# Attention stage: reductions over two PSUM banks, and a score ring of three banks in place of two pairs

## The chip, the cores and the metric

The kernel runs on one core of one Trainium2 chip. The metric is device time in microseconds; the kernel before took 2791.23 us (median of three runs, 2777.22 to 2791.93).

## The reference, cut to what matters

Sixteen images of 32 channels and 56 x 56 pixels go through a convolution block, a single-head self-attention over the 3136 pixels of each image, and a small mixture-of-experts layer. The change touches the attention alone:

```python
def _L1_attn_ref(x, Wq, bq, Wk, bk, Wv, bv):
    q = jnp.einsum('bsd,de->bse', x, Wq) + bq
    k = jnp.einsum('bsd,de->bse', x, Wk) + bk
    v = jnp.einsum('bsd,de->bse', x, Wv) + bv
    scores = jnp.einsum('bqd,bkd->bqk', q, k) / jnp.sqrt(d)
    attn = jax.nn.softmax(scores, axis=-1)
    return jnp.einsum('bqk,bkd->bqd', attn, v) + x
```

## The kernel before, in words

Three stages follow one another: `prepare` (convolutions, and the stacks of keys and queries, written to device memory), `attend`, and `finish` (value projection, experts, output). `attend` is the part of the change.

Per image the scores are laid out with keys on partitions: 24 full chunks of 128 keys and one of 64 (`NF` = 24), against seven tiles of 448 queries (`TILE`). Four kinds of work make up the stage.

- **Scores** (`scores`, matmuls on L1158): one matmul of 128 x 128 weights and 448 columns per chunk and tile, into the tensor `psS`. It holds four PSUM banks as two pairs; a pair is filled by two matmuls, and one ScalarE instruction over 896 columns (`exponentials`, L1248) takes the exponential of both and writes the ring `PR` in SBUF.
- **Maxima** (`maxima`, matmuls on L1182): the row maximum of the scores is needed ahead of the exponential, so the scores are computed a second time, with queries on partitions. Two matmuls that use 64 array rows each run beside each other, into two banks out of the three of `psX`; VectorE reduces each bank (448 columns) with an instruction of its own (L1331). An image has 172 such units, taken as 86 pairs. They run 32 pairs ahead of the scores (`LEAD`).
- **Sums** (`sums`, L1200): the exponentials times the values, four chunks at a time in four column strips of 32, fp32, accumulated in `psV`. Two matmul records stand for each product, eight for a step. At the end of a query tile four small products with the half chunk are added (L1207), and ScalarE copies `psV` out (`keep`, L1255).
- **Half chunks** (`half_scores`, L1147, and `half_exponentials`, L1241): the last 64 keys of two query tiles in one bank. They use a bank of the score pairs in turn. `max_parts` (L1342) and `turn_max` (L1192, L1350) bring the maxima of a part of an image into a row that the score matmuls subtract.

A **step** is four chunks of one query tile; an image has 42 steps, the stage 672. The order on TensorE is written out by hand in the last loop of its block. Each engine runs its instructions in order and waits on semaphores: `s_full` (scores there), `p_ready` (exponential done, so the bank is free), `x_full` and `x_done` for the maxima, `p_used` for the ring `PR`. The order of a step before is:

```python
scores(n, s, 0)                # two matmuls, one pair of banks
maxima(*pairs[0])
sums(*divmod(q, STEPS))        # of two steps earlier
half_scores(n, s // PSTEPS)    # only in 4 of 42 steps
maxima(*pairs[1])
scores(n, s, 1)                # the other pair
```

So the second pair of scores of a step and the first of the next stand together, four matmuls in a row. Of the 672 steps 625 hold two pairs of maxima, 31 hold three and one holds one; the last 15 hold none. A score pair waits until the exponential of the pair two places back is done; a pair of maxima waits until all but the last reduction of those issued ahead of it are done.

Of the kernel before, what the change touches and what calls it, by code (L numbers as in the profile page):

```python
# [10 lines left out]
ALU = mybir.AluOpType  # L11
# [935 lines left out]
def attend(nc, wts, scr, fin):  # L947
# [3 lines left out]
    with ExitStack() as ctx:  # L951
# [18 lines left out]
        SLOTS = 2 * STEPS + PARTS  # L970
# [5 lines left out]
        PRS = 8  # L976
# [5 lines left out]
        PR = sb("PR", [P, PRS, 2, TILE])  # L982
        PL = sb("PL", [P, PARTS, TILE])
        XM = sb("XM", [P, NT, NF])
        XE = sb("XE", [P, PARTS])
# [4 lines left out]
        psS = ps("psS", [P, 2, 2, 512])  # L990
        psX = ps("psX", [P, 3, 512])
# [25 lines left out]
        def place(m, i):  # L1017
            return (m * (UNITS + PARTS) + 2 * i + sum(last_pair(p) + DELAY < i for p in range(PARTS - 1))
                    - (m >= 1 and i < DELAY))

        def turn_place(m, p):
            if p < PARTS - 1:
                return place(m, last_pair(p) + DELAY) + 2
            return place(m + 1, DELAY - 1) + 2 if m + 1 < N else place(m, XPAIRS - 1) + 2
# [25 lines left out]
        def slot(n, s, j):  # L1050
            return n * SLOTS + 2 * s + s // PSTEPS + j + (s % PSTEPS > 0 or j == 1)

        def half_slot(n, p):
            return n * SLOTS + p * (2 * PSTEPS + 1) + 1

# [85 lines left out]
        def _(pe):  # L1141
            def half_scores(n, p):
                b, at = n % B, half_slot(n, p)
                if at >= 2:
                    pe.wait_ge(p_ready, at - 1)
                for h, t in enumerate(half_tiles(p)):
                    last = nc.tensor.matmul(psS[HALF * h:HALF * h + HALF, at % 2, 0, 0:TILE], KS[:, b, TF:T],  # L1147
# [3 lines left out]
            def scores(n, s, i):  # L1151
                b, at, (t, c) = n % B, slot(n, s, i), divmod(2 * s + i, NF // 2)
                if i == 0 and s % PSTEPS == 0:
                    pe.wait_ge(m_in, rows_in(n, s // PSTEPS))
                if at >= 2:
                    pe.wait_ge(p_ready, at - 1)
                for k in range(2):
                    last = nc.tensor.matmul(psS[:, at % 2, k, 0:TILE], KS[:, b, (2 * c + k) * P:(2 * c + k + 1) * P],  # L1158
                                            US[:, b, t * TILE:(t + 1) * TILE], start=True, stop=True)
                last.then_inc(s_full, 1)  # L1160

            def maxima(m, i):
# [7 lines left out]
                if at + 1 >= 3:  # L1170
                    pe.wait_ge(x_done, at - 1)
                for j in range(2):
# [3 lines left out]
                    o = psX[:, (at + j) % 3, 0:TILE]  # L1176
# [7 lines left out]
                    last.then_inc(x_full, 1)  # L1184
# [591 lines left out]
```

## Time and profile before

| what | value |
|---|---|
| median of three runs | 2791.23 us (2777.22 to 2791.93) |
| span of the profiled execution | 2788.9 us |
| TensorE busy | 2406.2 us, 86% |
| VectorE busy | 2339.7 us, 84% |
| ScalarE busy | 1600.3 us, 57% |
| GpSimd busy | 396.3 us, 14% |
| scoring stage (first score to last sum) | 583 to 2269.6 us |

The profiled execution has no time of its own beside its span; the span lies 2.3 us under the median of the runs and inside their range. Busy time of an engine is the time in which at least one of its instructions is in a record, so pipelined matmuls overlap in it. PE stands for TensorE's matmuls, PEld for its weight loads, DVE for VectorE, ACT for ScalarE.

### The profile page before, as it was taken

The page shows a single profiled execution, that of the slowest core. Times are in us where ns is not written, and L with a number is a line of the kernel's source. Part 1 is how long each engine was busy: PE and PEld are TensorE (multiplying, and loading weights), DVE is VectorE, ACT ScalarE, POOL GpSimd, SP SyncE. Part 2 cuts the span into 40 slices and gives each one's busy share as a digit, 9 for nine tenths or more (in the row PEclk, how much of TensorE's full clock was granted, in tenths as well). Part 3 has the DMA queues.
Part 4 walks back from the last instruction along what each step waited for, and adds up shares of the span by engine and source line. Part 5 has one row for each costly group of instructions (what it writes and reads, how often), then busy time and mean ns, then how long its engine had stood idle before and what let it go on. Part 6 is the DMA issues. An engine that isn't in the chain of part 4 may idle for free. (4 is left out here: it accounts for less than half of the span.)

```text
span 2788.9 us, 46984 instructions
## 1 busy us (share of the span) xinstructions
PE 2406.2 (86%) x18454; PEld 959.6 (34%) x18454; DVE 2339.7 (84%) x4150; ACT 1600.3 (57%) x2106; POOL 396.3 (14%) x456
## 2 busy tenths in 40 slices
PE   3888878379999999999999999999999987766775
PEld 1343333122222222222222222222222246655663
DVE  4567776699999999999999999999999927777777
ACT  1143343247777777777777777777777753233323
POOL 0021121300000000000000000000000004444445
PEclk9989989579999999999999999999999986666766
DMA  7687692500210230211211201201200011222221
GB/s 173 171 221 221 192 270 97 177 24 1 59 50 10 59 107 17 59 38 22 59 33 28 59 24 36 59 18 42 59 7 19 24 62 55 70 75 100 70 70 24
DMA packets 68110, 206.29 MB, mean 74 GB/s; under 512 B 20630, under 2 KB 33554, under 8 KB 61234
## 3 DMA queue, kind: packets, MB, share of 16 engines
q1 hardware_dynamic: 64034, 185.27, 24.1%
q0 software_dynamic: 3040, 15.57, 1.5%
q8 instruction: 145, 2.38, 0.4%
q10 hardware_dynamic: 816, 2.46, 0.3%
q14 instruction: 75, 0.61, 0.1%
HBM read 80.14 MB, written 61.31 MB: 51 GB/s over the span
## 5 line engine op out<-in xcount | busy, mean ns | idle before, releaser
L1331 DVE TENSOR_REDUCE at_XM<-at_psX 128x1 f32<-128x448 f32 x2688 | 1546.2, 620 | 90.1 <-PE at_psX L1182 69.3
L1248 ACT ACTIVATE at_PR<-at_psS 128x896 f32<-128x896 f32 x1344 | 1163.1, 915 | 452.3 <-PE at_psS L1158 450.3
L1200 PE MATMUL at_psV<-at_PR,at_V 128*32 128x448 f32 x5376 | 644.8, 551 | 0.1
L1158 PE MATMUL at_psS<-at_US,at_KS 128*128 128x448 f16 x2688 | 636.1, 356 | 0.6 <-ACT at_PR L1248 0.2
L1182 PE MATMUL at_psX<-at_KS,at_US 64*128 64x448 f16 x1344 | 490.2, 365 | 64.8 <-DVE at_XM L1331 42.9
L1182 PE MATMUL at_psX<-at_KS,at_UH 64*128 64x448 f16 x1344 | 490.3, 365 | 0.0
L1182 PEld LDWEIGHTS at_psX<-at_KS,at_US 64*128 64x128 f16 x1344 | 124.6, 93 | 720.5 <-DVE at_XM L1331 661.4
L1158 PEld LDWEIGHTS at_psS<-at_US,at_KS 128*128 128x128 f16 x2688 | 200.9, 98 | 273.1 <-ACT at_PR L1248 119.4
L1297 POOL CAST at_mrow<-at_mt 7x128 f16<-7x128 f32 x64 | 18.0, 281 | 1611.0 <-DVE at_mt L1350 1258.2
L1588 POOL TENSOR_TENSOR fi_WE<-fi_WE 128x256 f32<-128x256 f32 (+1 forms) x224 | 202.5, 935 | 179.7 <-DVE fi_WE L1641 179.6
L1641 DVE TENSOR_TENSOR fi_WE<-fi_psE,fi_WT 128x512 f32<-128x512 f32 (+1 forms) x208 | 134.2, 666 | 74.4 <-PE fi_psE L1495 73.3
L389 PE MATMUL psA<-sb_stacks,sb_lhs 128*32 128x448 f32 x1568 | 157.1, 547 | 0.8 <-DVE sb_X L841 0.8
L1200 PEld LDWEIGHTS at_psV<-at_PR,at_V 128*32 128x32 f32 x5376 | 105.8, 108 | 134.0 <-issue 126.5
L1474 PE MATMUL fi_psK<-fi_ident,fi_Z 128*128 128x128 f16 x400 | 55.7, 292 | 111.4 <-DVE fi_Z L1690 111.4
L1465 PE MATMUL fi_psO<-fi_wv,fi_SUMS 128*128 128x33 f32 x800 | 137.8, 347 | 7.5 <-PEq L951 6.4
L1465 PEld LDWEIGHTS fi_psO<-fi_wv,fi_SUMS 128*128 128x128 f32 x800 | 135.8, 270 | 10.5 <-issue 9.2
L1495 PE MATMUL fi_psE<-fi_wz,fi_ZS 128*128 128x256 f16 x400 | 108.8, 381 | 27.0 <-DVE fi_WE L1641 27.0
L1182 PEld LDWEIGHTS at_psX<-at_KS,at_UH 64*128 64x128 f16 x1344 | 124.6, 93 | 0.0
L1559 ACT ACTIVATE fi_SQ<-fi_XH 128x800 f32<-128x800 f32 x16 | 13.9, 870 | 185.5 <-DVE fi_XH L1672 185.5
L349 PE MATMUL psA<-sb_stacks,sb_lhs 128*32 128x448 f32 x448 | 56.1, 646 | 49.3 <-DMA sb_stacks<-sb_Xp 49.3
L678 POOL TENSOR_TENSOR sb_TK<-sb_TK,sb_XH 128x800 f32<-128x800 f32 x13 | 43.5, 3348 | 369.7 <-DVE sb_XH L787 369.7
L808 DVE SCALAR_TENSOR_TENSOR sb_X<-sb_T,sb_w7e,sb_X 128x3136 f32<-128x3136 f32 x20 | 69.8, 3488 | 28.8 <-ACT sb_T L508 28.0
(200 smaller groups left out, 2050.4 us busy)
## 6 DMA issues: line engine op xcount, KB each, us to landing
sums<-at_O SPq DMA_DIRECT2D x16, 1568.0 KB, 6.3
fi_SUMS<-sums SPq DMA_DIRECT2D x16, 1568.0 KB, 6.5
sb_stacks<-sb_T SPq DMA_DIRECT2D x64, 270.5 KB, 7.6
sb_stacks<-sb_Xp SPq DMA_DIRECT2D x64, 248.8 KB, 9.7
sb_stacks<-sb_Xp SPq DMA_DIRECT2D x64, 248.0 KB, 5.8
sb_stacks<-sb_T SPq DMA_DIRECT2D x64, 172.5 KB, 10.8
at_KS<-key_stacks SPq DMA_DIRECT2D x32, 208.0 KB, 6.8
fi_RES<-residual SPq DMA_DIRECT2D x16, 400.0 KB, 7.0
```

Of the source, the lines that this page charges most:

```text
L349: last = nc.tensor.matmul(psA[C * n:C * n + C, i % 2, 0:TILE], lhs2[:, j, :], xrows(XS[:, n], XTOP + TR * i, XLEFT - 1 + j), start=(j == 0 ...
L389: last = nc.tensor.matmul(o, w, v, start=(j == 0), stop=(j == 6))
L808: last = nc.vector.scalar_tensor_tensor(out=x3, in0=yrows(T2[:], YTOP, i, H), scalar=w7e[:, i:i + 1], in1=x3, op0=ALU.mult, op1=ALU.add)
L1158: last = nc.tensor.matmul(psS[:, at % 2, k, 0:TILE], KS[:, b, (2 * c + k) * P:(2 * c + k + 1) * P], US[:, b, t * TILE:(t + 1) * TILE], sta ...
L1182: last = nc.tensor.matmul(o, u[:, c * P:(c + 1) * P], k[:, t * TILE:(t + 1) * TILE], start=True, stop=True)
L1200: last = nc.tensor.matmul(psV[C * q:C * q + C, 0:TILE], V[:, b, G * k + q, :], PR[:, (n * 2 * STEPS + 2 * q4 + q // 2) % PRS, q % 2, :], s ...
L1248: nc.scalar.activation(PR[:, f % PRS], psS[:, at % 2, :, 0:TILE], ACT.Exp).then_inc(p_ready, 1)
L1331: nc.vector.tensor_reduce(o, psX[:, (at + j) % 3, 0:TILE], AX.X, ALU.max).then_inc(x_done, 1)
L1465: last = nc.tensor.matmul(psO[:, h, q * (C + 1):(q + 1) * (C + 1)], SUMS[:, b, a:a + P], wv[:], start=True, stop=True)
L1495: last = nc.tensor.matmul(psE[:, u % 2, j * EC:(j + 1) * EC], ZS[:, b, a:a + P], wz16[:, 0:EC], start=True, stop=True)
L1588: return nc.gpsimd.tensor_tensor(WE[:, s, 0:h, 0:w], WE[:, s, 0:h, 0:w], WE[:, s, h:2 * h, 0:w], ALU.add)
L1641: nc.vector.tensor_tensor(WE[:, u // 2, :, q:q + j].rearrange("p e k c -> p k e c"), psE[:, u % 2, 0:j * EC].rearrange("p (k e c) -> p k e ...
```

## The change

1. `psX` becomes two pairs of banks (four banks). A pair of maxima is one place (`x_full`, `x_done` count pairs), and one VectorE instruction reduces both banks: 128 x 2 results from 128 x 896 inputs. The results lie in a flat `XM` of 172 columns.
2. `psS` becomes a ring of three single banks, which frees the bank that `psX` takes. Each score matmul has a place of its own. The exponentials take the banks 0 and 1 of the ring together (896 columns) and bank 2 alone (448 columns). The table `group_of` lays this down: 896 instructions over two banks, 896 over one, and 64 half chunks alone, where there were 1344 over two and 64 half chunks. A score matmul waits for the group that holds the bank's previous contents.
3. TensorE's order within a step becomes score, maxima, score, sums, (half), score, maxima, score.
4. `PR` has 16 single slots in place of 8 double ones (same size). ScalarE copies `psV` out behind the fourth score of the step, where it stood behind the first two.

The core of the diff:

```diff
-        PRS = 8
+        PRS = 16
+        SBANKS = 3
...
-        psS = ps("psS", [P, 2, 2, 512])
-        psX = ps("psX", [P, 3, 512])
+        psS = ps("psS", [P, SBANKS, 512])
+        psX = ps("psX", [P, 2, 2, 512])
...
+        while len(group_of) < N * (QUAD + PARTS):
+            at, g = len(group_of), group_of[-1] + 1 if group_of else 0
+            two = (at + 1 < N * (QUAD + PARTS) and not is_half(at) and not is_half(at + 1)
+                   and at % SBANKS < SBANKS - 1 and fulls % PRS < PRS - 1)
+            fulls += 0 if is_half(at) else 1 + two
+            group_of += [g] * (1 + two)
...
+            def scores(n, s, k):
+                b, at, (t, c) = n % B, score_place(n, s, k), divmod(4 * s + k, NF)
...
+                if at >= SBANKS:
+                    pe.wait_ge(p_ready, groups_to(at - SBANKS))
+                nc.tensor.matmul(psS[:, at % SBANKS, 0:TILE], KS[:, b, c * P:(c + 1) * P],
+                                 US[:, b, t * TILE:(t + 1) * TILE], start=True, stop=True).then_inc(s_full, 1)
...
                     scores(n, s, 0)
                     if len(pairs) >= 1:
                         maxima(*pairs[0])
-                    q = n * STEPS + s - LAG
+                    scores(n, s, 1)
                     if q >= 0:
                         sums(*divmod(q, STEPS))
                     if s % PSTEPS == 0:
                         half_scores(n, s // PSTEPS)
+                    scores(n, s, 2)
                     if len(pairs) >= 2:
                         maxima(*pairs[1])
-                    scores(n, s, 1)
+                    scores(n, s, 3)
                     if len(pairs) >= 3:
                         maxima(*pairs[2])
...
-            def exponentials(n, s, i):
+            def exponentials(n, s, k):
+                at, f = score_place(n, s, k), n * QUAD + 4 * s + k
+                if not ends_group(at):
+                    return
+                w = 1 if starts_group(at) else 2
                 act.wait_ge(s_full, at + 1)
                 if f >= PRS:
-                    act.wait_ge(p_used, (f - PRS) // 2 + 1)
-                nc.scalar.activation(PR[:, f % PRS], psS[:, at % 2, :, 0:TILE], ACT.Exp).then_inc(p_ready, 1)
+                    act.wait_ge(p_used, (f - PRS) // 4 + 1)
+                r, bank = f % PRS - w + 1, at % SBANKS - w + 1
+                nc.scalar.activation(PR[:, r:r + w], psS[:, bank:bank + w, 0:TILE], ACT.Exp).then_inc(p_ready, 1)
...
-                for j in range(2):
-                    c, t = unit(2 * i + j)
-                    dve.wait_ge(x_full, at + j + 1)
-                    o = XE[:, t:t + 1] if c == NF else XM[:, t, c:c + 1]
-                    nc.vector.tensor_reduce(o, psX[:, (at + j) % 3, 0:TILE], AX.X, ALU.max).then_inc(x_done, 1)
+                dve.wait_ge(x_full, at + 1)
+                nc.vector.tensor_reduce(XM[:, 2 * i:2 * i + 2], psX[:, at % 2, :, 0:TILE], AX.X, ALU.max).then_inc(x_done, 1)
```

## Rows read from the trace of the kernel before

**Rows 1.** Page, first line: span of the profiled execution.

```profile
span 2788.9 us, 46984 instructions
```

**Rows 2.** Windows view of the stage. Columns: stretch, busy us per engine, clock.

```profile
583.00:2269.60 1686.60, 1650.87 (x11903) 476.10 (x11902) 1573.01 (x2848) 1257.80 (x1519) 81.61 (x147) 1.00 0.14 37
```

**Rows 3.** Timeline, one ordinary step. Columns: start, length, engine, line, operation.

```profile
1195.23 0.93 PE L1158 MATMUL at_psS<-at_US,at_KS 128*128 128x448 f16 x4
...
1195.82 1.73 ACT L1248 ACTIVATE at_PR<-at_psS 128x896 f32<-128x896 f32 x2 [0.62 <-PE at_psS L1158]
...
1196.09 0.36 PE L1182 MATMUL at_psX<-at_KS,at_US 64*128 64x448 f16 x1
...
1196.39 0.96 PE L1200 MATMUL at_psV<-at_PR,at_V 128*32 128x448 f32 x8
...
1197.27 0.09 PEld L1182 LDWEIGHTS at_psX<-at_KS,at_US 64*128 64x128 f16 x1 [0.73 <-DVE at_XM L1331]
...
1197.57 0.49 PEld L1158 LDWEIGHTS at_psS<-at_US,at_KS 128*128 128x128 f16 x4 [0.20 <-ACT at_PR L1248]
```

**Rows 4.** Timeline, narrower, inside one burst of four score matmuls.

```profile
1202.26 0.93 PE L1158 MATMUL at_psS<-at_US,at_KS 128*128 128x448 f16 x4
...
1202.65 0.54 PE L1158 MATMUL at_psS<-at_US,at_KS 128*128 128x448 f16 x2
```

**Rows 5.** Groups by line, 800:1900. Last columns: busy us, mean ns, idle before.

```profile
L1331 DVE TENSOR_REDUCE at_XM<-at_psX 128x1 f32<-128x448 f32 x1753 | 1008.3, 620 | 48.0 <-PE at_psX L1182 36.4
...
L1341 DVE TENSOR_REDUCE at_negm<-at_XE 128x1 f32<-128x4 f32 x10 | 1.6, 158 | 0.3
...
L1248 ACT ACTIVATE at_PR<-at_psS 128x896 f32<-128x896 f32 x878 | 759.7, 914 | 260.0 <-PE at_psS L1158 258.5
...
L1241 ACT ACTIVATE at_PL<-at_psS 128x448 f32<-128x448 f32 x41 | 22.3, 544 | 13.5 <-PE at_psS L1147 13.5
```

**Rows 6.** Timeline, 1204.7 to 1205.5: a score matmul that waits for ScalarE.

```profile
1204.73 0.54 ACT L1241 ACTIVATE at_PL<-at_psS 128x448 f32<-128x448 f32 x1 [0.15 <-PE at_psS L1147]
...
1205.32 0.11 PEld L1158 LDWEIGHTS at_psS<-at_US,at_KS 128*128 128x128 f16 x2 [0.30 <-ACT at_PL L1241]
...
1205.50 0.92 ACT L1248 ACTIVATE at_PR<-at_psS 128x896 f32<-128x896 f32 x1 [0.23 <-PE at_psS L1158]
```

**Rows 7.** Timeline, a run of reductions without a gap.

```profile
1223.78 14.03 DVE L1331 TENSOR_REDUCE at_XM<-at_psX 128x1 f32<-128x448 f32 x24 [0.22 <-PE at_psX L1182]
```

**Rows 8.** Timeline and windows: maxima alone, and two stretches with a lower clock.

```profile
550.03 0.10 PEld L1182 LDWEIGHTS at_psX<-at_KS,at_US 64*128 64x128 f16 x1 [1.17 <-DVE at_XM L1331]
...
545.00:575.00 30.00, 13.26 (x48) 2.44 (x48) 27.34 (x49) 0.00 (x0) 0.00 (x0) 0.50 0.51 134
...
2400.00:2500.00 100.00, 71.93 (x555) 62.32 (x554) 75.23 (x150) 29.97 (x45) 46.66 (x47) 0.67 0.22 73
```

**Rows 9.** Timeline, 2240.9 to 2242.7: steps without maxima.

```profile
2240.91 0.96 PE L1200 MATMUL at_psV<-at_PR,at_V 128*32 128x448 f32 x8
...
2242.17 0.11 PEld L1158 LDWEIGHTS at_psS<-at_US,at_KS 128*128 128x128 f16 x2 [0.27 <-ACT at_PR L1248]
...
2242.66 0.96 PE L1200 MATMUL at_psV<-at_PR,at_V 128*32 128x448 f32 x8
```

**Rows 10.** Timeline, the sums (L1200) of six steps in a row, 1210 to 1225.

```profile
1210.98 0.96 PE L1200 MATMUL at_psV<-at_PR,at_V 128*32 128x448 f32 x8
...
1213.93 0.96 PE L1200 MATMUL at_psV<-at_PR,at_V 128*32 128x448 f32 x8
...
1216.27 0.96 PE L1200 MATMUL at_psV<-at_PR,at_V 128*32 128x448 f32 x8
...
1219.61 0.96 PE L1200 MATMUL at_psV<-at_PR,at_V 128*32 128x448 f32 x8
...
1222.30 0.96 PE L1200 MATMUL at_psV<-at_PR,at_V 128*32 128x448 f32 x8
...
1224.83 0.96 PE L1200 MATMUL at_psV<-at_PR,at_V 128*32 128x448 f32 x8
```

More of the change, by code:

```diff
@@ L969, in attend @@
         PSTEPS = 2 * QUADS
-        SLOTS = 2 * STEPS + PARTS
+        QUAD = 4 * STEPS
         UNITS = NF * NT + PARTS
@@ L1017, in place @@
         def place(m, i):
-            return (m * (UNITS + PARTS) + 2 * i + sum(last_pair(p) + DELAY < i for p in range(PARTS - 1))
+            return (m * (XPAIRS + PARTS) + i + sum(last_pair(p) + DELAY < i for p in range(PARTS - 1))
                     - (m >= 1 and i < DELAY))
@@ L1047, in first_pairs, with score_place, half_place, is_half @@
             return [divmod(g, XPAIRS) for g in range(LEAD)]
[L1050 to L1054, printed above, removed]
+        def score_place(n, s, k):
+            return n * (QUAD + PARTS) + 4 * s + s // PSTEPS + k + (s % PSTEPS > 0 or k >= 2)
+        def half_place(n, p):
+            return n * (QUAD + PARTS) + p * (4 * PSTEPS + 1) + 2
+        def is_half(at):
+            n, r = divmod(at, QUAD + PARTS)
+            return r in [half_place(0, p) for p in range(PARTS)]
+        def ring_of(n, s, k):
+            return (n * QUAD + 4 * s + k) % PRS
+        group_of = []
+        fulls = 0
+        while len(group_of) < N * (QUAD + PARTS):
[4 more added lines that the diff above has]
+            group_of += [g] * (1 + two)
+        def groups_to(at):
+            return group_of[at] + 1
+        def ends_group(at):
+            return at + 1 == len(group_of) or group_of[at + 1] > group_of[at]
+        def starts_group(at):
+            return at == 0 or group_of[at - 1] < group_of[at]
         def half_tiles(bank):
@@ L1142, in half_scores @@
             def half_scores(n, p):
[L1143 to L1145 removed]
+                b, at = n % B, half_place(n, p)
+                if at >= SBANKS:
+                    pe.wait_ge(p_ready, groups_to(at - SBANKS))
                 for h, t in enumerate(half_tiles(p)):
[L1147 removed]
+                    last = nc.tensor.matmul(psS[HALF * h:HALF * h + HALF, at % SBANKS, 0:TILE], KS[:, b, TF:T],
                                             US[:, b, t * TILE:(t + 1) * TILE], start=True, stop=True)
                 last.then_inc(s_full, 1)
[L1151 to L1153 removed]
+            def scores(n, s, k):
+                b, at, (t, c) = n % B, score_place(n, s, k), divmod(4 * s + k, NF)
+                if k == 0 and s % PSTEPS == 0:
                     pe.wait_ge(m_in, rows_in(n, s // PSTEPS))
[L1155 to L1160, printed above, removed]
+                if at >= SBANKS:
+                    pe.wait_ge(p_ready, groups_to(at - SBANKS))
+                nc.tensor.matmul(psS[:, at % SBANKS, 0:TILE], KS[:, b, c * P:(c + 1) * P],
+                                 US[:, b, t * TILE:(t + 1) * TILE], start=True, stop=True).then_inc(s_full, 1)
             def maxima(m, i):
@@ L1199, in sums @@
                 for q in range(G):
-                    last = nc.tensor.matmul(psV[C * q:C * q + C, 0:TILE], V[:, b, G * k + q, :],
-                                            PR[:, (n * 2 * STEPS + 2 * q4 + q // 2) % PRS, q % 2, :], start=(k == 0),
-                                            stop=(k == QUADS - 1))
+                    last = nc.tensor.matmul(psV[C * q:C * q + C, 0:TILE], V[:, b, G * k + q, :], PR[:, ring_of(n, q4, q)],
+                                            start=(k == 0), stop=(k == QUADS - 1))
                 last.then_inc(p_used, 1)
@@ L1258, in _ @@
                 for s in range(STEPS):
-                    exponentials(n, s, 0)
+                    for k in range(4):
+                        if k == 2 and s % PSTEPS == 0:
+                            half_exponentials(n, s // PSTEPS)
+                        exponentials(n, s, k)
                     m, q4 = divmod(n * STEPS + s - LAG, STEPS)
```

42 lines of the change are left out of this document (20 added, 22 removed).

## The prediction

> **What bounds the kernel now.** I read the page first: a span of 2788.9 us [rows 1]. The windows view then cuts out the scoring stage: from 583 to 2269.6 us, 1686.6 us, TensorE is busy 1650.9, VectorE 1573.0 and ScalarE 1257.8, at a granted clock of 1.00 (2.4 GHz) [rows 2]. Two engines are nearly full, so a saving on one alone is worth nothing until it is known which of them sets the pace. The timeline of one step tells it [rows 3]. I call a score matmul S, a pair of maxima M, the piece of sums SUM. Starts on TensorE: four S at 1195.23, M at 1196.09, SUM at 1196.39, M at 1197.27, the next four S at 1197.57. So four S take 0.86 us, M 0.29 or 0.30, SUM 0.89, M 0.29, together 2.34 to 2.35.
>
> Are these work or waits? The weight loads of the second M and of the S are put down to VectorE (0.73 idle) and ScalarE (0.20) [rows 3], but those labels name only the latest event ahead. Inside a burst the third S starts 0.39 after the first, 0.195 each [rows 4]; a pair of S with nothing to wait for hands over to SUM after 0.49 [rows 9], four after 0.86 [rows 3], so a further S costs 0.19 and every change to another kind of work 0.10 to 0.12. M (0.19 + 0.10), SUM (0.79 + 0.10) and the burst (0.76 + 0.10) then leave no room for a wait. **TensorE issues without a gap; it sets 2.345 us a step.** VectorE is just beside it: 24 reductions in a row take 14.03 us, so the 23 before the last are (14.03 - 0.62) / 23 = 0.583 each [rows 5, 7], and four are 2.33. ScalarE is not: two exponentials over two banks take 1.73 us of the step, 0.815 from start to start and 0.915 to the end of one [rows 3, 5].
>
> As a check I add the stage up. SUM to SUM over steps in a row [rows 10]: ordinary 2.34 (from 1213.93), with a turned maximum 2.95, with a third pair 3.34, with a half chunk 2.69, with the half products at a tile's end 2.53. By the counts in the program: 657 x 2.345 = 1541; 15 steps without maxima at 1.76 [rows 9], 26; 64 turns x 0.60, 38; 31 third pairs x 1.00, 31; 64 halves x 0.35, 22; 112 tile ends x 0.19, 21. That is 1679 of the measured 1686.6, so the step model holds to 0.5%.
>
> **The change, part by part.**
>
> *One reduction over two banks.* VectorE: 448 columns take 620 ns, 4 columns 158 ns [rows 5], so 1.04 ns a column, and 896 take 620 + 466 = 1086 ns, 1.05 from start to start where two took 1.166. No row shows a VectorE instruction across two banks; the bounds are 1.05 and, if it gained nothing, 1.24 (two rows of 620). I take 1.05, as ScalarE's row over two banks shows no extra at the seam (914 ns for 896 columns, 544 for 448 [rows 5]). 1376 pairs x 0.116 = 160 us less work for VectorE, but TensorE sets the pace, so it is worth nothing in ordinary steps. It counts in the lead of 32 pairs, at 1.27 each now (0.10 + 1.17 [rows 8]): -7 us; in third pairs (1.00 each now, as a reduction is then late; after it some 0.35 of TensorE's time): 31 x 0.65 = -20; and in turns (0.60 now, some 0.30 after): 64 x 0.30 = -19.
>
> *TensorE's order.* Before: a burst of four, M, SUM, M: four changes of kind. After: S3 and the next S0 together 0.49, M 0.29, S 0.30, SUM 0.89, S 0.30, M 0.29 = 2.56 us, six changes of kind. By this alone a step is 0.22 us longer.
>
> Why a change of kind costs anything decides whether it also does so for a single S. The rows show 0.10 whatever the pair of kinds [rows 3, 9]. The Trainium skill ("TensorEngine Tiling (Array Packing)", Key Properties) says that changing the tiling mode drains TensorE. S (128 x 128), M (64 x 128) and SUM (128 x 32) are three modes, so the rule speaks against this change; the trace agrees in kind, with 0.10 us. Taken as a drain to the end of the record (0.353 - 0.19 = 0.16 us) the two added changes would be 0.32 a step, not 0.20.
>
> *The ring of three.* Four more durations: a matmul that really waits starts 0.05 after the exponential ends (1204.73 + 0.54 = 1205.27, load at 1205.32 [rows 6]); an exponential starts 0.40 after the start of the last S that it reads (third S 1195.23 + 0.19 = 1195.42 for the second of the pair, exponential at 1195.82 [rows 3]); E2, over two banks, frees them 0.915 after its start and holds ScalarE 0.815; E1, over one, 0.544 [rows 5] and 0.44 (0.815 less 448 columns at 0.83 ns). Places repeat every 12 scores, three steps. Starts, from S0 = 0:
>
> - Step A: S0 0, M 0.30, S1 0.59 (E2 of banks 0, 1 at 0.99, free at 1.96), SUM 0.89, S2 1.78 (E1 2.18, free 2.77), M 2.08, S3 2.37.
> - Step B: S4 2.56 (E2 2.96, free 3.93), M 2.86, S5 3.15 (E1 behind E2, 3.78, free 4.37), SUM 3.45, S6 4.34, M 4.64, S7 4.93 (E2 5.33, free 6.30).
> - Step C: S8 5.12 (E1 6.15, free 6.74), M 5.42, S9 could start at 5.71 but needs bank 0: 6.30, a wait of 0.59. SUM 6.60, S10 7.49 (E2 7.89, free 8.85), M 7.79, S11 8.08; the next S0 could start at 8.27, needs bank 0: 8.85, a wait of 0.58.
>
> 8.85 us for three steps is 2.95 a step, 0.605 more than 2.345. The cause is visible in C: S9 and S10 are read by one exponential, and the SUM of 0.89 stands between them, so bank 0 lies full and unread for a microsecond. Before, the two matmuls of one exponential always followed at once. VectorE in this schedule has 1.47 us for each pair and needs 1.05 (even 1.24 fits), so M never waits. 657 x 0.605 = **+397 us**. The same schedule without M gives 7.67 us for three steps, 2.56 each; before 1.76 [rows 9]: 15 x 0.80 = +12.
>
> *The rest.* The half products of 112 tile ends cost 0.19 now, where the next M has some slack, and 0.31 on a path without slack: +13. Half chunks: 0.35 now; after it between 0.30 (TensorE's time alone) and 0.74 (a third of a ring turn of 2.21 us); I take 0.50, near the middle: 64 x 0.15 = +10 (-3 to +25). The copy of `psV` on ScalarE (0.44) now precedes an exponential that is on the path in two of three phases, by some 0.1: 112 x 0.1 = +11 (0 to +49). `PR` holds four steps as before and sums lag by two: no wait there, 0. Two or one group more per ring turn on ScalarE (1856 instructions for 1408) fill its idle time, already in the schedule.
>
> Sum: 397 - 7 - 20 - 19 + 12 + 13 + 10 + 11 = +397 us. The other stages are untouched. Against the profiled span this gives 3186; the span stands 2.3 us under the median, so **3188 us**. The small terms cancel to nothing; the forecast is the ring.
>
> **Rivals.**
>
> - *Only TensorE's order counts* (0.12): the two ring waits vanish, because a bank is freed sooner than the rows say. 657 x 0.22 = +145, the small terms 0: 2936 us. For it: it needs no chain through ScalarE. Against: the wait of S9 follows from the program, E2 of S6 and S7 can't end before both are in.
> - *A single S between others hides the change of kind* (0.06): with 0.19 for each S the same schedule gives 8.08 us for three steps (the waits of S9 and S0 grow to about 0.7 as TensorE arrives earlier), 2.69 a step: 657 x 0.35 = +230: 3021 us. Against: none of the changes in rows 3 and 9 is free.
> - *VectorE was the bound* (0.04; the other side): its 0.583 a reduction sets the step, TensorE's apparent lack of gaps is chance, and TensorE fits in the shorter step. 1376 x 0.116 = -160: 2631 us. It decides from the point where TensorE's new order and the ring need less than 2.345 us a step. For it: 24 reductions with no gap [rows 7], the labels of rows 3. Against: 2.56 us of TensorE work in the new order.
> - *No change, the two effects cancel* (0.02): 2791 us.
> - *The clock falls* (0.06): in the lead, with TensorE busy 13.3 of 30 us, it is 0.50 (1.2 GHz), in the last stage, busy 71.9 of 100, 0.67 on the mean [rows 8]; the new step idles 1.17 of 8.85 us. At 1.2 GHz a step's 4 S, 2 M and SUM would take 1.87 us more; over a tenth of the steps +123: 3309 us.
>
> The drain to the record's end would add 657 x 0.12 = 79 us to the forecast, by the Trainium skill's rule ("TensorEngine Tiling (Array Packing)", Key Properties) read at its hardest: 3267 us. It holds no chance of its own, as rows 3 show 0.10.
>
> **How the numbers follow.** The forecast has 0.70: 3188 us, of which the unknown sizes (half chunks, copy, turns, the release time: 0.02 us more or less on a ring turn is 18 us over 900 turns) make 3120 to 3255. The range takes in the second rival and goes a little of the way to the clock's: 2990 to 3270, with some 0.78 inside. What a measurement tells from no change is 0.5%, 14 us. Faster: 0.04; within 0.5%: 0.02; slower: 0.70 + 0.12 + 0.06 + 0.06 = 0.94.
>
> **What would show it.** In the profile after: VectorE's two-bank row near 1086 ns, and VectorE's share in the stage down to some 70%; in the timeline single S with 0.30 to the next kind; S9 and the next S0 with waits for `at_PR` near 0.6 us, and a period of 8.85 us over three steps; ScalarE rows of 915 and 544 in turn, with idle before them put down to S; the stage ending some 397 us later with the clock still at 1.00. A stage step under 2.6 us would make the ring argument wrong; one under 2.345 would show that VectorE had set the pace.

## The result and the profile after

The changed kernel takes 3176.9 us (median of four runs, 3168.7 to 3187.0), the kernel before 2791.6: a ratio of 1.1425, 95% interval 1.1371 to 1.148. The forecast was 3188 us. The profiled execution's span is 3178.2 us, 389.3 over [rows 1].

The stage, in the windows view (stretch, its length, busy us and count for PE, PEld, DVE, ACT, POOL, then clock), against 1650.9, 1573.0 and 1257.8 busy of 1686.6 [rows 2]:

```profile
583.00:2660.00 2077.00, 1822.11 (x11844) 499.54 (x11848) 1447.38 (x1499) 1316.17 (x1958) 81.35 (x147) 1.00 0.11 30
```

VectorE is busy for 126 us less in this window (121 us less over the whole stage, 576.5 to 2665.7) and now fills 70% of it, at the same granted clock of 1.00 (2.4 GHz). The stage is longer all the same. The groups by line and shape, 543 to 2700 us (busy us, mean ns | idle before, releaser), beside [rows 5]:

```profile
L1357 DVE TENSOR_REDUCE at_XM<-at_psX 128x2 f32<-128x896 f32 x1376 | 1454.6, 1087 | 601.2 <-PE at_psX L1206 582.2 <-PE at_psX L1203 18.3
...
L1277 ACT ACTIVATE at_PR<-at_psS 128x896 f32<-128x896 f32 x896 | 821.9, 917 | 703.8 <-PE at_psS L1183 701.9
L1277 ACT ACTIVATE at_PR<-at_psS 128x448 f32<-128x448 f32 x896 | 484.6, 541 | 79.9 <-PE at_psS L1183 76.5
```

Both engines that read PSUM wait for TensorE: VectorE 601 us (48 of 1100 us were shown before [rows 5]), ScalarE 704 ahead of its two-bank instructions and 80 ahead of the others. That split fits the ring: it is the pair of scores that comes late.

The order of starts on TensorE over three steps without a half chunk or a third pair, from the timeline (start, length; the second matmul of a pair of maxima, on UH, is left out), answers to [rows 3] and to the list in the prediction:

```profile
1317.45 0.36 PE L1183 MATMUL at_psS<-at_US,at_KS 128*128 128x448 f16 x1 [0.42 <-ACT at_PR L1277]
1317.74 0.36 PE L1206 MATMUL at_psX<-at_KS,at_US 64*128 64x448 f16 x1
...
1318.04 0.36 PE L1183 MATMUL at_psS<-at_US,at_KS 128*128 128x448 f16 x1
1318.33 0.96 PE L1224 MATMUL at_psV<-at_PR,at_V 128*32 128x448 f32 x8
1319.22 0.36 PE L1183 MATMUL at_psS<-at_US,at_KS 128*128 128x448 f16 x1
1319.52 0.36 PE L1206 MATMUL at_psX<-at_KS,at_US 64*128 64x448 f16 x1
...
1319.82 0.55 PE L1183 MATMUL at_psS<-at_US,at_KS 128*128 128x448 f16 x2
1320.30 0.36 PE L1206 MATMUL at_psX<-at_KS,at_US 64*128 64x448 f16 x1
...
1320.60 0.36 PE L1183 MATMUL at_psS<-at_US,at_KS 128*128 128x448 f16 x1
1320.89 0.96 PE L1224 MATMUL at_psV<-at_PR,at_V 128*32 128x448 f32 x8
1321.78 0.36 PE L1183 MATMUL at_psS<-at_US,at_KS 128*128 128x448 f16 x1
1322.08 0.36 PE L1206 MATMUL at_psX<-at_KS,at_US 64*128 64x448 f16 x1
...
1322.37 0.55 PE L1183 MATMUL at_psS<-at_US,at_KS 128*128 128x448 f16 x2
1322.86 0.36 PE L1206 MATMUL at_psX<-at_KS,at_US 64*128 64x448 f16 x1
...
1323.74 0.36 PE L1183 MATMUL at_psS<-at_US,at_KS 128*128 128x448 f16 x1 [0.53 <-ACT at_PR L1277]
...
1324.93 0.36 PE L1183 MATMUL at_psS<-at_US,at_KS 128*128 128x448 f16 x1
...
1326.30 0.36 PE L1183 MATMUL at_psS<-at_US,at_KS 128*128 128x448 f16 x1 [0.42 <-ACT at_PR L1277]
```

From S0 at 1317.45 the forecast's 0.30, 0.59, 0.89, 1.78, 2.08, 2.37 stand as 0.29, 0.59, 0.88, 1.77, 2.07, 2.37. S9 comes at 6.29 (forecast 6.30), behind an idle array, S10 at 7.48 (7.49), and the next S0 at 8.85 (8.85). Between S9 and S10 stands the piece of sums; until S10 is in, nobody reads bank 0. The idle times in brackets (0.42 and 0.53) count from the end of the row before, which is 0.36 us long, while the next matmul of a kind follows after 0.20 and one of another kind after 0.30; so they stand for delays of 0.58 and 0.59 us.

### The profile page after: what moved, and what is told of

It reads as the page before. It is cut to its first block and busy times, and to the rows that moved or that the text cites. A ratio compares the mean times of both kernels' runs of the same rounds, so it can differ in the third digit from the quotient of the medians.

```text
span 3178.2 us, 46502 instructions
## 1 busy us (share of the span) xinstructions
PE 2584.1 (81%) x18454; PEld 982.8 (31%) x18454; DVE 2210.2 (70%) x2774; ACT 1665.0 (52%) x2554; POOL 395.6 (12%) x456
## 5 line engine op out<-in xcount | busy, mean ns | idle before, releaser
L1357 DVE TENSOR_REDUCE at_XM<-at_psX 128x2 f32<-128x896 f32 x1376 | 1454.6, 1087 | 601.2 <-PE at_psX L1206 582.2
L1277 ACT ACTIVATE at_PR<-at_psS 128x896 f32<-128x896 f32 (+1 forms) x1792 | 1250.4, 729 | 783.8 <-PE at_psS L1183 778.4
L1183 PE MATMUL at_psS<-at_US,at_KS 128*128 128x448 f16 x2688 | 895.5, 362 | 201.8 <-ACT at_PR L1277 200.8
L1206 PE MATMUL at_psX<-at_KS,at_US 64*128 64x448 f16 x1344 | 489.8, 365 | 48.0 <-DVE at_XM L1357 27.6
L1183 PEld LDWEIGHTS at_psS<-at_US,at_KS 128*128 128x128 f16 x2688 | 227.3, 96 | 929.9 <-ACT at_PR L1277 501.9
L1206 PE MATMUL at_psX<-at_KS,at_UH 64*128 64x448 f16 x1344 | 489.8, 365 | 0.0
L1326 POOL CAST at_mrow<-at_mt 7x128 f16<-7x128 f32 x64 | 17.9, 279 | 1992.2 <-DVE at_mt L1378 1544.5
L1206 PEld LDWEIGHTS at_psX<-at_KS,at_US 64*128 64x128 f16 x1344 | 124.5, 93 | 395.6 <-issue 305.5
L1493 PE MATMUL fi_psO<-fi_wv,fi_SUMS 128*128 128x33 f32 x800 | 128.6, 332 | 7.6 <-PEq L951 6.4
L1493 PEld LDWEIGHTS fi_psO<-fi_wv,fi_SUMS 128*128 128x128 f32 x800 | 126.5, 253 | 10.8 <-issue 9.2
L1206 PEld LDWEIGHTS at_psX<-at_KS,at_UH 64*128 64x128 f16 x1344 | 124.6, 93 | 0.0
```

The lines of the kernel that those rows point to most:

```text
L1183: nc.tensor.matmul(psS[:, at % SBANKS, 0:TILE], KS[:, b, c * P:(c + 1) * P], US[:, b, t * TILE:(t + 1) * TILE], start=True, stop=True).the ...
L1206: last = nc.tensor.matmul(o, u[:, c * P:(c + 1) * P], k[:, t * TILE:(t + 1) * TILE], start=True, stop=True)
L1277: nc.scalar.activation(PR[:, r:r + w], psS[:, bank:bank + w, 0:TILE], ACT.Exp).then_inc(p_ready, 1)
L1357: nc.vector.tensor_reduce(XM[:, 2 * i:2 * i + 2], psX[:, at % 2, :, 0:TILE], AX.X, ALU.max).then_inc(x_done, 1)
L1493: last = nc.tensor.matmul(psO[:, h, q * (C + 1):(q + 1) * (C + 1)], SUMS[:, b, a:a + P], wv[:], start=True, stop=True)
```

## The experiments

Several theories go into them. Mine: the loss is a sum of TensorE's order (two more changes of kind, 0.22 us a step) and of waits of the three-bank ring under two-bank exponentials (0.39 us), VectorE nowhere. The rivals: the order alone, the number of banks whatever is done with them, or VectorE. Times are medians of four runs; the kernel before, run on the same chips, stood at 2784.2 us (b_order, d_dve2, c_adj, a_singles), 2780.6 (g_keep, e_twos, the two with threes), 2783.9 (k_keep, j_mm) and 2782.8 (l_spread, of ten runs itself, and m_spread_dve2). Each ratio is against it.

| kernel | median us | ratio (95%) |
|---|---|---|
| the change | 3176.9 | 1.1425 (1.1371 to 1.148) |
| k_keep: its copy earlier | 3157.3 | 1.135 (1.1308 to 1.1393) |
| d_dve2: two reductions | 3194.1 | 1.1466 (1.1436 to 1.1497) |
| b_order: before, new order | 3114.9 | 1.1186 (1.1161 to 1.121) |
| c_adj: sums behind the pair | 3060.2 | 1.0995 (1.0973 to 1.1016) |
| a_singles: one-bank exponentials | 2983.1 | 1.0713 (1.0687 to 1.0739) |
| h_threes_keep | 2927.5 | 1.0519 (1.0475 to 1.0564) |
| f_threes: bursts of three | 2924.0 | 1.0514 (1.0475 to 1.0553) |
| g_keep: a_singles, copy earlier | 2917.7 | 1.0498 (1.0472 to 1.0524) |
| e_twos: bursts of two | 2868.0 | 1.0323 (1.0293 to 1.0353) |
| j_mm: maxima side by side | 2834.6 | 1.0192 (1.0156 to 1.0227) |
| m_spread_dve2: two reductions | 2827.3 | 1.0152 (1.0122 to 1.0181) |
| l_spread: j_mm, extras moved | 2785.1 | 1.0013 (0.9988 to 1.0038) |

**a_singles: every exponential takes one bank.**

```diff
-                   and at % SBANKS < SBANKS - 1 and fulls % PRS < PRS - 1)
+                   and False)
```

> The changed kernel, but every exponential takes one bank (2688 ScalarE instructions over 448 columns and 64 half chunks); TensorE's order and VectorE's two-bank reductions stay. My theory (TensorE's order costs 0.22 us a step, the ring with two-bank exponentials 0.39): a bank is now free 0.40 + 0.54 + 0.05 = 1.0 us after its score matmul starts, and the same bank is asked for 1.8 us or more later, so the ring waits go and a step takes 2.56 us: 2791 + 657 x 0.22 = about 2935 us (2900 to 2970). Rival, the three banks are too few whatever the grouping: the time stays near 3177 us. Rival, ScalarE's instructions bound it (0.44 us each, 1.76 a step, plus copies): that is under 2.56, so it would only show above 3000 us. Rival, a single score matmul between other work costs nothing extra: 2791 us or less.

Measured 2983 us, 194 less than the change, with the same order, banks and reductions and with 896 more ScalarE instructions. TensorE's row of waits for the exponential, 178.7 us between 583 and 2480 in the changed kernel, is down to 3.3. So with this order three banks are enough when each is read by itself, and it was the pairing that cost. It is 48 us above my number. The waits view (in total, times, longest) of TensorE's matmuls in this kernel, 583 to 2480 us, names a candidate:

```profile
PE at_psV L1224 <- ACT at_O L1284: 42.0, 110, 0.6
PE at_psX L1216 <- DVE at_XM L1357: 29.4, 47, 0.9
PE at_psX L1206 <- DVE at_XM L1357: 18.9, 46, 0.6
```

**g_keep: a_singles with the copy of the finished sums behind the second score's exponential.**

```diff
                         exponentials(n, s, k)
-                    m, q4 = divmod(n * STEPS + s - LAG, STEPS)
-                    if m >= 0 and q4 % QUADS == QUADS - 1:
-                        keep(m, q4 // QUADS)
+                        m, q4 = divmod(n * STEPS + s - LAG, STEPS)
+                        if k == 1 and m >= 0 and q4 % QUADS == QUADS - 1:
+                            keep(m, q4 // QUADS)
```

> The changed kernel with one-bank exponentials, and the copy of the finished sums on ScalarE put behind the second score's exponential of the step (where it stood before the change), in place of behind the fourth. The run with one-bank exponentials came out some 45 us above my 2935; its trace has TensorE's sums waiting 42.0 us for this copy, 110 times. Theory: the place of the copy is that remainder; moved, those waits go and the time falls by about 40 us to 2943 us (2930 to 2955). Rival, the copy only hides another wait (VectorE's turned maxima, or the next exponential behind a copy that waits for the sums): 2975 to 2985 us.

Measured 2918 us, 65 less, more than the 42 of waits. The copy's place was the remainder and somewhat more. In the traces a step at a tile's end falls from 3.20 to 2.75 us, 0.45 at each of 108 such steps, 48 us; the stage as a whole is 55 us shorter, and the last stage, which is the same in both, 8 us. This kernel is the cleanest measure of the order, as almost no wait for ScalarE is left in it (3.9 us for the exponentials, none for the copy): 137 us over the kernel before, where the prediction had put the order at 145.

**k_keep: the same move of the copy in the changed kernel** (the diff of g_keep on it).

> The changed kernel as it is, two-bank and one-bank exponentials, with only the copy of the finished sums put back behind the second score's exponential of the step. With one-bank exponentials this gave 65 us. In the changed kernel's trace TensorE waits some 13 us for that copy and ScalarE's ring is on the path. Theory (ring turn decides, the copy costs what I had put at 11 us, or up to 0.44 us at each of 112 tile ends): 3177 less 10 to 50 us, 3125 to 3165 us. Rival, the copy's place is a large part of the change's loss, as large as with one-bank exponentials or larger: below 3115 us. Rival, it is hidden in the ring waits: 3177 us.

Measured 3157 us, 20 less, inside the first expectation. With ring waits still there, most of the copy's cost is covered by them.

**b_order: the kernel before with only TensorE's order changed.** The two matmuls of a score pair become two calls, the wait before the first and the signal on the second.

```diff
-                    scores(n, s, 0)
+                    scores(n, s, 0, 0)
                     if len(pairs) >= 1:
                         maxima(*pairs[0])
+                    scores(n, s, 0, 1)
...
+                    scores(n, s, 1, 0)
                     if len(pairs) >= 2:
                         maxima(*pairs[1])
-                    scores(n, s, 1)
+                    scores(n, s, 1, 1)
```

> The kernel before (four score banks in two pairs, three banks for the maxima, two reductions for a pair of maxima), with one thing of the change: TensorE's order score, maxima, score, sums, score, maxima, score. It measures the two added changes of kind alone. My theory: six changes of kind in place of four, a step of 2.56 us for 2.345, +145 us, less some 20 to 40 us because VectorE is no longer late at third pairs and turns: 2895 to 2940 us, no waits on ScalarE. Rival, changes of kind cost nothing when the matmul between them is single: 2791 us. Rival, the whole loss is the order, the ring none: 3177 us.

Measured 3115 us: a miss of about 190, above my range and 62 us under the second rival. The timeline of TensorE shows what I had left out:

```profile
1305.14 0.36 PE L1157 MATMUL at_psS<-at_US,at_KS 128*128 128x448 f16 x1
1305.44 0.36 PE L1182 MATMUL at_psX<-at_KS,at_US 64*128 64x448 f16 x1
...
1305.73 0.55 PE L1157 MATMUL at_psS<-at_US,at_KS 128*128 128x448 f16 x2
1306.51 0.36 PE L1182 MATMUL at_psX<-at_KS,at_US 64*128 64x448 f16 x1 [0.23 <-DVE at_XM L1333]
...
1306.81 0.36 PE L1157 MATMUL at_psS<-at_US,at_KS 128*128 128x448 f16 x1
1307.10 0.96 PE L1200 MATMUL at_psV<-at_PR,at_V 128*32 128x448 f32 x8
1307.99 0.36 PE L1157 MATMUL at_psS<-at_US,at_KS 128*128 128x448 f16 x1
```

A step takes 2.85 us (1305.14 to 1307.99). The new order puts the maxima of one step and the first of the next only two scores apart. With three banks, a pair of maxima waits until the first reduction of the pair ahead is done, 0.40 + 0.62 + 0.05 = 1.07 us after its start, and that is what stands there (1305.44 to 1306.51); TensorE would have come at 0.78. The wait of 0.29 us a step is 657 x 0.29 = 190 us, the whole miss. So the new order needs the two bank pairs for the maxima, which the changed kernel has: there the same distance is 0.78 (1319.52 to 1320.30) with no wait. The doubled banks do carry their weight, but against a cost that the order brings.

**c_adj: in the changed kernel, the sums stand behind the third score wherever the second and third are read together.**

```diff
+                    joined = not starts_group(score_place(n, s, 2)) and s % PSTEPS > 0
...
                     scores(n, s, 1)
-                    if q >= 0:
+                    if q >= 0 and not joined:
                         sums(*divmod(q, STEPS))
...
                     scores(n, s, 2)
+                    if q >= 0 and joined:
+                        sums(*divmod(q, STEPS))
```

> The changed kernel, with the sums put behind the third score of the step wherever the second and third are read by one exponential (one step in three); nothing else is moved and the number of changes of kind falls by one in those steps at most. My theory: the exponential of that pair starts 0.9 us earlier, the wait at the next step's first score (0.58 us every three steps) goes, a period of three steps falls from 8.85 to about 8.17 us: 3177 - 657 x 0.227 = 3028 us (2990 to 3060), with the wait at the ninth score left. Rival, the ring does not matter and only TensorE's work counts: one hand-over fewer in three steps is 0.1 us, 22 us in all, 3155 us.

Measured 3060 us, 117 less (expected 149, rival 22). Moving one thing in one step of three returns 117 us. About 22 of them are the hand-over that goes with it, by the rival's price; the rest is the exponential that no longer waits behind the sums. Its timeline:

```profile
1340.92 0.55 PE L1183 MATMUL at_psS<-at_US,at_KS 128*128 128x448 f16 x2 [0.52 <-ACT at_PR L1280]
1341.41 0.96 PE L1224 MATMUL at_psV<-at_PR,at_V 128*32 128x448 f32 x8
1342.30 0.36 PE L1206 MATMUL at_psX<-at_KS,at_US 64*128 64x448 f16 x1
...
1342.59 0.55 PE L1183 MATMUL at_psS<-at_US,at_KS 128*128 128x448 f16 x2
```

S9 and S10 go together, S11 and the next S0 follow without a wait, S0 at 1342.78, 1.86 after S9 as worked out (1.87). The wait at S9 stays. Of the 32 us that are missing, the waits view from 583 to 2480 us shows some 21: TensorE's waits for the copy are 20.8 us for 11.9, for VectorE 47.3 for 35.6. The rest is open.

**d_dve2: the changed kernel with two reductions of 448 columns for each pair.**

```diff
-                nc.vector.tensor_reduce(XM[:, 2 * i:2 * i + 2], psX[:, at % 2, :, 0:TILE], AX.X, ALU.max).then_inc(x_done, 1)
+                nc.vector.tensor_reduce(XM[:, 2 * i:2 * i + 1], psX[:, at % 2, 0, 0:TILE], AX.X, ALU.max).then_inc(x_half, 1)
+                nc.vector.tensor_reduce(XM[:, 2 * i + 1:2 * i + 2], psX[:, at % 2, 1, 0:TILE], AX.X, ALU.max).then_inc(x_done, 1)
```

> The changed kernel with two VectorE instructions of 448 columns for a pair of maxima, in place of one of 896. My theory: VectorE has 1.47 us for each pair in the changed kernel and needs 1.17, so only the lead gets longer (32 x 0.12 = 4 us): 3180 us, within 10 of the changed kernel, VectorE busier by some 160 us. Rival, VectorE is on the path somewhere in each step: up to 1376 x 0.116 = 160 us more, 3337 us.

Measured 3194 us, 17 above the change's median, with ratios whose intervals overlap. In the two traces the stage, from the first score to the last product of a half chunk, takes 2103.8 us for 2089.2, 15 more. So the two-bank instruction is worth some 15 us here, not 160. VectorE is busy for 2298.9 us of the execution in place of 2210.2, 89 more where I had expected 160. The groups by line show the two, 529.6 us of idle time left ahead of them:

```profile
L1357 DVE TENSOR_REDUCE at_XM<-at_psX 128x1 f32<-128x448 f32 x1376 | 853.4, 620 | 529.6 <-PE at_psX L1206 511.4 <-PE at_psX L1203 16.0
L1358 DVE TENSOR_REDUCE at_XM<-at_psX 128x1 f32<-128x448 f32 x1376 | 843.7, 613 | 0.0
```

The rest start from a_singles and look for an order that pays.

**e_twos: score, score, maxima, score, score, sums, maxima.**

```diff
                     scores(n, s, 0)
+                    scores(n, s, 1)
                     if len(pairs) >= 1:
                         maxima(*pairs[0])
-                    scores(n, s, 1)
-                    if q >= 0:
-                        sums(*divmod(q, STEPS))
                     if s % PSTEPS == 0:
                         half_scores(n, s // PSTEPS)
                     scores(n, s, 2)
+                    scores(n, s, 3)
+                    if q >= 0:
+                        sums(*divmod(q, STEPS))
                     if len(pairs) >= 2:
                         maxima(*pairs[1])
-                    scores(n, s, 3)
```

> The changed kernel with one-bank exponentials and TensorE's order score, score, maxima, (half), score, score, sums, maxima: five changes of kind a step in place of six. By hand: 0.49 + 0.29 + 0.49 + 0.89 + 0.29 = 2.45 us, with a wait of 0.03 for the first bank's release (1.0 us after its score matmul started), 2.48 us a step: 2790 + 657 x 0.135 - 46 (lead, third pairs, turns) + 13 = about 2846 us (2820 to 2880). Rival, bursts of two run into the ring of three more than that (the fourth score asks for the first one's bank 0.97 us later): above 2900 us. Rival, the changes of kind are not the price of the order: no gain over one-bank exponentials alone, 2983 us.

Measured 2868 us, within the expectation and 22 above its middle: the third pairs and turns, of which I had counted on 39 us, give nothing back here either (see the table below). The steps have the 2.48 us that were worked out, by the sums in its timeline:

```profile
1325.89 0.96 PE L1224 MATMUL at_psV<-at_PR,at_V 128*32 128x448 f32 x8
...
1328.37 0.96 PE L1224 MATMUL at_psV<-at_PR,at_V 128*32 128x448 f32 x8
```

**f_threes: scores in bursts of three, one pair of maxima behind each, and where due the sums and a second pair.**

```diff
+            for i in range(0, len(line), 3):
+                for n, s, k in line[i:i + 3]:
...
+                due = min(LEAD + full * XPAIRS / (4 * STEPS), N * XPAIRS)
+                if pair < due:
+                    maxima(*divmod(pair, XPAIRS))
+                    pair += 1
+                if full >= 4 * (quad + LAG) + 2:
+                    sums(*divmod(quad, STEPS))
+                    quad += 1
+                    if pair < due:
+                        maxima(*divmod(pair, XPAIRS))
+                        pair += 1
```

> The changed kernel with one-bank exponentials and scores in bursts of three, as many as the ring has banks; behind each burst a pair of maxima, and where due a piece of sums and a second pair. By hand for 12 scores, three steps: 4 x 0.68 + 6 x 0.29 + 3 x 0.89 = 7.13 us, 2.38 a step beside 2.345 before: 657 x 0.035 = +23, less 46 us of VectorE's lateness at the lead, third pairs and turns: about 2770 us (2750 to 2830), the first version that could be level with the kernel before. Rival, the short turns (a burst and one pair of maxima, 0.97 us) meet banks freed only 1.0 us after their score, and ScalarE needs 1.32 us for three: waits of 0.1 to 0.4 us in one turn of four, up to 2860 us. Rival, VectorE's two-bank reduction is late where maxima stand close together: above 2860 us.

Measured 2924 us, worse than bursts of two and past the first rival's 2860. The number lies in the range of the second rival, but its mechanism does not show: TensorE's matmuls wait 13 us for VectorE's reductions between 583 and 2480 us. The first rival was right in kind: in the timeline a burst behind a turn without sums takes 1.17 us (1319.82 to 1320.99) where one with free banks takes 0.68 (1322.84 to 1323.52).

```profile
1319.82 1.24 PE L1183 MATMUL at_psS<-at_US,at_KS 128*128 128x448 f16 x3
1320.99 0.36 PE L1206 MATMUL at_psX<-at_KS,at_US 64*128 64x448 f16 x1
...
1322.84 0.74 PE L1183 MATMUL at_psS<-at_US,at_KS 128*128 128x448 f16 x3
1323.52 0.36 PE L1206 MATMUL at_psX<-at_KS,at_US 64*128 64x448 f16 x1
```

Such a turn comes once in three steps or so: (0.49 / 3) x 657 = 107 us of the 154 missed. I had not put the 1.32 us of three exponentials into the sum, only into the rival.

**h_threes_keep: f_threes with the copy behind the third score** (`k == 2` in the diff of g_keep).

> As the run with bursts of three, with the copy of the finished sums one exponential earlier on ScalarE (behind the third score of the step). Theory: up to 0.4 us less at each of 112 tile ends, 0 to 45 us less than the bursts of three alone. Rival: the copy waits for the sums and holds the next exponential back, which costs as much: within 10 us, or slower.

Measured 2927 us, 4 from f_threes: the rival. The copy now waits itself for the sums (ScalarE's waits for `psV` are 55.7 us for 21.8, 583 to 2480 us), and TensorE's waits for the exponentials grow from 19.7 to 32.0 us while the 17.9 for the copy go.

**j_mm: score, score, maxima, maxima, score, score, sums.**

```diff
                     scores(n, s, 0)
+                    scores(n, s, 1)
...
+                    for pair in pairs:
+                        maxima(*pair)
                     scores(n, s, 2)
                     scores(n, s, 3)
+                    if q >= 0:
+                        sums(*divmod(q, STEPS))
```

> The changed kernel with one-bank exponentials and TensorE's order score, score, (half), maxima, maxima, score, score, sums: four changes of kind a step, as before the change. By hand: 0.49 + 0.49 + 0.49 + 0.89 = 2.36 us for TensorE. The second pair of maxima needs the bank pair that VectorE reduces last: 0.40 + 1.05 + 1.09 + 0.05 = 2.59 us after the first of the step before, so 2.40 us a step. Against bursts of two (2.48): 657 x 0.08 = 53 us less, about 2815 us (2795 to 2845), still behind the kernel before, whose step is 2.345. Rival, VectorE is now late at every turn and third pair with both pairs of maxima side by side: no gain over bursts of two, 2868 us or more. Rival, it beats the kernel before (2784): only if the turns and third pairs give back more than the 46 us I count.

Measured 2835 us, 34 less than bursts of two (53 expected), within the range. An ordinary step takes 2.36 us (sums at 1322.46 and 1324.82), with the two pairs of maxima 0.20 apart and no 0.10 between them. But TensorE waits for VectorE where a third pair or a turned maximum follows at once. Waits view, TensorE's matmuls, 583 to 2480 us, and one of the places:

```profile
PE at_psX L1206 <- DVE at_XM L1353: 73.6, 78, 1.0
...
PE at_psX L1216 <- DVE at_XM L1353: 14.9, 15, 1.0
```

```profile
1339.60 0.36 PE L1206 MATMUL at_psX<-at_KS,at_US 64*128 64x448 f16 x1
...
1339.81 0.36 PE L1206 MATMUL at_psX<-at_KS,at_US 64*128 64x448 f16 x1
...
1341.15 0.36 PE L1206 MATMUL at_psX<-at_KS,at_US 64*128 64x448 f16 x1 [0.98 <-DVE at_XM L1353]
```

**l_spread: j_mm, with what goes beyond two places for maxima in a step moved behind the sums.** `items` holds the step's pairs of maxima and its turned maximum, in order.

```diff
-                    for pair in pairs:
-                        maxima(*pair)
+                    for item in items[:2]:
+                        item()
                     scores(n, s, 2)
                     scores(n, s, 3)
                     if q >= 0:
                         sums(*divmod(q, STEPS))
+                    for item in items[2:]:
+                        item()
```

> The order score, score, (half), maxima, maxima, score, score, sums, with whatever goes beyond two places for maxima in a step (a third pair, a turned maximum and what follows it) put behind the sums. In the run without that (2835 us) TensorE's steps take 2.36 us, and it waits 88.5 us for VectorE, in pieces of 0.98 and 0.99 us, at third pairs and turns. Theory: they are what keeps that kernel behind the kernel before (2784 us); 0.9 us of sums and 0.5 us of scores later the banks are free, so some 60 to 80 us of the waits go and 95 more changes of kind cost 0.1 to 0.2 us each: 2775 to 2795 us, level with the kernel before. Rival, VectorE has no room (2.1 of 2.36 us a step), the waits only move to the next maxima: 2820 to 2840 us.

Measured 2785 us against 2783, ratio 1.0013 (0.9988 to 1.0038): level with the kernel before, as worked out. The waits fall from 88.5 to 35.6 us (22.6 at L1206, 13.0 at the turned maxima, 583 to 2400 us). The layout of the change is thus not what loses 385 us: with one-bank exponentials, the copy and this order it loses nothing. It also wins nothing.

**m_spread_dve2: l_spread with the two reductions of d_dve2.**

> As the run above, with two reductions of 448 columns for each pair in place of one of 896. In the changed kernel that cost 0 to 17 us. Theory: VectorE's saving counts as soon as TensorE's step is short; here the second pair of maxima waits for the last reduction of the step before, 0.40 + 1.17 + 1.20 + 0.05 = 2.82 us after the first, 0.2 us behind which it starts: 2.62 us a step for 2.40, 657 x 0.22 = 145 us more than the run above. Rival, TensorE bounds it all the same: under 40 us more.

Measured 2827 us, 42 above l_spread, not 145. VectorE's saving does count once TensorE's step is short, but a number of mine was wrong. Its timeline on VectorE, one reduction a line:

```profile
1320.90 0.63 DVE L1360 TENSOR_REDUCE at_XM<-at_psX 128x1 f32<-128x448 f32 x1 [0.57 <-PE at_psX L1206]
1321.44 0.61 DVE L1361 TENSOR_REDUCE at_XM<-at_psX 128x1 f32<-128x448 f32 x1
1321.97 0.61 DVE L1360 TENSOR_REDUCE at_XM<-at_psX 128x1 f32<-128x448 f32 x1
1322.50 0.61 DVE L1361 TENSOR_REDUCE at_XM<-at_psX 128x1 f32<-128x448 f32 x1
```

Reductions over one bank follow each other after 0.53 us, not 0.583, and two over two banks take 2.09 in l_spread, 1.00 from start to start:

```profile
1326.08 2.09 DVE L1360 TENSOR_REDUCE at_XM<-at_psX 128x2 f32<-128x896 f32 x2 [0.26 <-PE at_psX L1206]
```

So the 24 reductions in 14.03 us [rows 7] ran at TensorE's pace: a row of 0.62 us hides gaps of 0.05 when starts are 0.583 apart. The second pair of maxima is due 0.40 + 1.07 + 1.14 + 0.05 = 2.66 us after the first of the step before, 0.1 later than TensorE's 2.36 + 0.20; 657 times up to 0.1 us is 66, and 42 were measured: the mean ordinary step grows from 2.351 us in l_spread to 2.424 here, some 2.48 and some still 2.35.

## Why the prediction was right

The means of all steps of a kind, from one piece of sums to the next, in the traces of three kernels (us):

| step | count | before | change | g_keep |
|---|---|---|---|---|
| ordinary | 406 | 2.34 | 2.96 | 2.56 |
| at a tile's end | 93 | 2.54 | 3.32 | 2.75 |
| with a half chunk | 62 | 2.69 | 3.26 | 2.87 |
| with a turned maximum | 46 | 2.89 | 3.25 | 3.24 |
| with a third pair | 15 | 3.34 | 3.33 | 3.33 |
| with both | 16 | 4.12 | 4.47 | 4.47 |

- *TensorE sets the pace before.* No run changes VectorE's work alone in the kernel before. What shows it is that 400 of its 406 ordinary steps take 2.34 us, the sum of TensorE's own pieces, while VectorE's four reductions need 2.12 to 2.14 (m_spread_dve2), and that TensorE's added 0.22 us comes back in every ordinary step of g_keep (2.56), where VectorE has less to do than before.
- *VectorE "just beside it" was wrong.* The 0.583 us a reduction was TensorE's pace seen in VectorE's rows; VectorE's own is 0.53 to 0.54 (m_spread_dve2), so four take 2.14 of the 2.345 us. The change saves 1.07 - 1.00 = 0.07 us a pair, 96 us in all, not 0.116 and 160. Neither was in the sum for ordinary steps, so the forecast did not pay for it; the rival "VectorE was the bound" was overpriced by it.
- *A change of kind costs 0.10 us.* The single scores of the changed kernel hand over after 0.29 to 0.30, as the bursts did. The order alone was put at +145 us; g_keep, without ring and copy waits, measures +137. The table says what is in it: 0.22 us in each ordinary step, some 142 us, and nothing back from third pairs and turns. Above ordinary steps these cost 69 us in all before and 74 in g_keep.
- *The ring.* Forecast 657 x (0.605 - 0.22) = 253 us for the waits. a_singles takes 194 us away, but brings waits of its own for the copy (42.0 us) in exchange; with them moved (g_keep) against the changed kernel with the same copy (k_keep) the difference is 3157 - 2918 = 240 us. Three steps take 8.85 us in the rows shown, to the hundredth; the mean ordinary step gives 8.87.
- *VectorE's row.* 1086 ns forecast, 1087 measured.
- *Third pairs and turns: mis-sized.* The sum had -39 us for them. In the changed kernel they cost 44 us above ordinary steps for 69 before, -25. A third pair alone came out as forecast (0.37 us, forecast 0.35) and so did a turn (0.30), but where both fall into one step it is 1.52 us and not 0.65. And these gains hang on the slow ring more than on VectorE's saving: with a step of 2.56 us in g_keep a turn costs 0.69, more than the 0.55 before, and both together 1.91. That is part of the misses of e_twos and f_threes, whose sums took 46 us off.
- *The forecast is within 11 us with some luck.* From the table, against the sum: ordinary steps 657 x 0.615 = +404 (397), third pairs and turns -25 (-39), half chunks -3 (+10), tile ends with the copy +18 (+24), steps without maxima +11 (+12), the lead -8 (-7). The ring is right by itself; the small terms miss by up to 14 us each and cancel.
- *The stage.* Its end moved from 2269.3 to 2665.6 us (last products of half chunks), +396, where the sum said +397. The first score came 6.4 us earlier (582.9 to 576.5; forecast 7); from the first pair of maxima to the first score it is 8.3 us less, 1.00 us a pair in place of 1.27. The forecast put this down to the two-bank instruction, but d_dve2, with two reductions a pair, needs only 1.06. So 0.21 of the 0.27 us come from the second pair of banks and 0.06 from the instruction. Its timeline on VectorE in the lead:

```profile
544.92 0.61 DVE L1357 TENSOR_REDUCE at_XM<-at_psX 128x1 f32<-128x448 f32 x1
...
545.98 0.61 DVE L1357 TENSOR_REDUCE at_XM<-at_psX 128x1 f32<-128x448 f32 x1
```

- *Sizes that were off.* The copy: put at +11 us (0 to 49), it is 20 in the changed kernel (k_keep) and 65 once the ring waits are gone. The last stage, which I called untouched, is 7 us shorter in this trace (512.6 for 519.6 from the stage's end to the last instruction); in the traces of all these kernels, whose last stage is the same, it takes 505 to 520 us, so this is no effect of the change that these runs can tell from scatter. The medians differ by 385 where the spans differ by 389.
- *Rivals.* The order alone (2936) is refuted by the waits in the rows after, which a_singles and c_adj take away, hidden changes of kind by the 0.29 to 0.30 of single scores, VectorE as the bound (2631) by the result itself and by d_dve2, a falling clock by the 1.00 of the stage.

For b_order I had not checked the maxima's ring against the new order and was 190 us off; each order needs its own check against every ring.

## What to carry to other kernels

Where an engine's starts follow each other by stream time plus hand-over, write down its order with the price of each hand-over, and then check every bank ring against it: a bank is held from its own matmul until the whole instruction that reads it ends, so whatever stands between two matmuls of one reader holds the first one's bank as well. With few banks it can pay to read them one at a time, with more instructions on an engine that has room. A saving on the second-busiest engine is worth what the busiest one lets through, and labels of waits in a trace that name it are no evidence that it is the bound.

## What the runs showed of the hardware

- A VectorE maximum over two PSUM banks takes 1087 ns for 896 columns, beside 620 for 448, with no cost at the seam; from start to start 1.00 us beside 2 x 0.53. The fixed part that such an instruction saves is 0.07 us, not what the lengths of the rows suggest (2 x 620 - 1087 = 153 ns).
- Two row-tiled pairs of matmuls one behind the other start 0.20 us apart, without the 0.10 of a change of kind (j_mm, 1339.60 and 1339.81).
